# Token lists in 64-byte lines that carry the entry's weight, with bounded gathers and scatters

## The reference

```python
# x: 16 x 112 x 512, ctx: 16 x 375 x 512, mask: 16 x 375
x = x + attention(layernorm(x), ctx, mask)         # one head, softmax over the 375 rows of ctx
h = layernorm(x).reshape(-1, 512)                  # 1792 tokens
probs = softmax(h @ gate_weight.T)                 # 64 experts
top_val, top_idx = top_k(probs, 8)
top_val = top_val / sum(top_val)
# an expert that is nobody's first four may be replaced by a similar one (mapping of 64 entries)
for each of the 1792 * 8 = 14336 entries (token, expert):
    gu = h[token] @ gate_up[expert].T              # 512 -> 2 x 192
    y = (silu(gu[:192]) * gu[192:]) @ down[expert].T
    out[token] += top_val * y
x = x + out
```

## Time and profile before

| | us |
|---|---|
| median of 3 runs (lowest to highest) | 867.94 (867.48 to 870.99) |
| the profiled execution, its own time | 862.66 |
| its span, first to last instruction | 860.9 |
| PE busy in the span | 693.2 (81%) |
| DVE busy | 528.5 (61%) |
| ACT busy | 459.6 (53%) |
| POOL busy | 516.5 (60%) |
| moved by DMA | 196.36 MB |

### The profile page before, as it was taken

The page is one execution under the profiler, slowest core; times in us unless marked ns, Lnnn a source line. Parts: engine busy times, 40 slices in busy tenths (PEclk is TensorE's granted clock), DMA queues, the critical chain, the costliest instruction groups (busy, mean ns, idle before and its releaser), DMA issues. The chain is left out here.

```text
span 860.9 us, 15404 instructions
## 1 busy us (share of the span) xinstructions
PE 693.2 (81%) x4264; PEld 566.3 (66%) x4264; DVE 528.5 (61%) x1291; ACT 459.6 (53%) x900; POOL 516.5 (60%) x515
## 2 busy tenths in 40 slices
PE   5986868676017999999999999988998899999740
PEld 2544545343016999988888888877887778778630
DVE  4755736464125677776677777676776776776620
ACT  3543434232004676667666666767666676666520
POOL 2053535646716588888786676667676666666440
PEclk9997978885557999999999999999999999999965
DMA  8999986972047899999999999999999999999767
GB/s 274 351 333 157 214 189 132 182 201 64 2 143 232 192 256 264 248 259 263 248 245 276 269 271 275 286 242 273 279 248 253 269 265 265 256 249 260 152 120 164
DMA packets 103382, 196.36 MB, mean 228 GB/s; under 512 B 27697, under 2 KB 27825, under 8 KB 102850
## 3 DMA queue, kind: packets, MB, share of 16 engines
q1 hardware_dynamic: 70098, 121.70, 50.0%
q0 software_dynamic: 33200, 73.68, 40.7%
HBM read 147.23 MB, written 51.77 MB: 231 GB/s over the span
## 5 line engine op out<-in xcount | busy, mean ns | idle before, releaser
L1232 PE MATMUL bank<-xh,w1h 128*128 128x256 f32 (+7 forms) x768 | 227.7, 296 | 12.7 <-issue 4.5
L1233 PE MATMUL bank<-xl,w1h 128*128 128x256 f32 (+7 forms) x768 | 219.7, 286 | 0.0
L1234 PE MATMUL bank<-xh,w1l 128*128 128x256 f32 (+7 forms) x768 | 219.7, 286 | 0.0
L611 POOL DMA_INDIRECT xg<-normed_tokens,list x145 | 156.0, 1076 | 64.6 <-issue 49.3
L593 POOL DMA_INDIRECT list_table<-token,slot x112 | 107.5, 960 | 123.7 <-DVE token L781 91.3
L1232 PEld LDWEIGHTS bank<-xh,w1h 128*128 128x128 f32 x768 | 146.3, 190 | 17.2 <-issue 16.0
L635 POOL DMA_INDIRECT out_rows<-ys,list x73 | 117.4, 1608 | 62.1 <-ACT ys L1055 45.9
L635 POOL DMA_INDIRECT second_sum<-ys,list x70 | 111.9, 1599 | 59.7 <-ACT ys L1055 37.2
L1233 PEld LDWEIGHTS bank<-xl,w1h 128*128 128x128 f32 x768 | 146.5, 191 | 0.0
L1234 PEld LDWEIGHTS bank<-xh,w1l 128*128 128x128 f32 x768 | 146.3, 190 | 0.0
L925 DVE TENSOR_TENSOR xl<-bank,xh 128x448 fp32r<-128x448 f32 (+3 forms) x145 | 84.2, 617 | 90.0 <-ACT xh L1063 65.9
(11 more groups left out here) (205 smaller groups left out, 1123.9 us busy)
## 6 DMA issues: line engine op xcount, KB each, us to landing
raw<-in_w SPq DMA_DIRECT2D x195, 256.0 KB
raw<-in_w2a SPq DMA_DIRECT2D x65, 256.0 KB
ctxT_s<-in_ctxT SPq DMA_DIRECT2D x16, 768.0 KB
ctx_s<-in_ctx SPq DMA_DIRECT2D x16, 768.0 KB
raw<-in_w2b SPq DMA_DIRECT2D x65, 128.0 KB
second_sum<-zeros SPq DMA_DIRECT2D x18, 256.0 KB
x_in<-in_x SPq DMA_DIRECT2D x16, 224.0 KB
out_rows<-x SPq DMA_DIRECT2D x16, 224.0 KB
```

The source lines that it names most:

```text
L611: pool.indirect_dma_start(xg[u.on(XGS)][0:u.m, t, :], None, normed, bass.IndirectOffsetOnAxis(ap=lists[u.on(LISTS)][0:u.m, t:t + 1], axis= ...
L1232: pe.matmul(bank[m][:, 0:W], wh, mh, start=(c == 0), stop=False)
L1233: pe.matmul(bank[m][:, 0:W], wh, ml, start=False, stop=False)
L1234: mm = pe.matmul(bank[m][:, 0:W], wl, mh, start=False, stop=(c == DK - 1))
```

## The change

An entry of a list is now a line of 16 words (64 bytes): word 0 is the token's number, word 1 the weight of the entry. `place_entries` finds the weight of each of the 8 entries by comparing all 64 positions with the 8 sorted ones, and `spread` and `publish` move it along with the position. The column of weights beside the normalized row, its store and POOL's `weights` are gone; ACT takes the scale of a row from the list in SBUF. Gathers and scatters of the 63 units name a bound (`bounds_check=TOK - 1`), above which a row is left out; the three gather buffers are cleared once at the start so that rows left out hold numbers. A tile's rows are now consecutive entries of the list. The fills of the lists are 16 times larger for each entry; a first part (640 lines of each list) is issued in slot 1, the rest in slots 2 to 7, and `enter` of batch 5 waits for it. The core of the diff:

```diff
-LIST_PARTS = (2048, 192)
+LIST_PARTS = (2048, 16)
-FILLED = 2048
+FILLED = 1920
+LINE = 16
+BLANKS = 128
+NEAR = 640
...
-    table = nc.dram_tensor("list_table", (PAD_LIST + PADS, 1), I32, kind="Internal").ap()
+    table = nc.dram_tensor("list_table", (PAD_LIST + BLANKS, LINE), I32, kind="Internal").ap()
-    normed = nc.dram_tensor("normed_tokens", (ROWS, ROW), F32, kind="Internal").ap()
+    normed = nc.dram_tensor("normed_tokens", (ROWS, D), F32, kind="Internal").ap()
...
-            def store_weights(b):
-                sp.wait_ge(c_place, b.n * PLACE + 1)
-                sp.dma_start(normed[b.n * T:(b.n + 1) * T, D:ROW], wd[b.on(STORED)][:]).then_inc(wd_out[b.on(STORED)], 16)
+            def fill_lists(i, done):
+                quarter = P // (PADS // BLANKS)
+                source = blank[i % (PADS // BLANKS) * quarter:(i % (PADS // BLANKS) + 1) * quarter].rearrange("p n c -> p (n c)")
+                per_expert = table[0:PAD_LIST].rearrange("(e n) c -> e (n c)", e=E)
+                for e in range(0, E, quarter):
+                    sp.dma_start(per_expert[e:e + quarter, i * BLANKS * LINE:(i + 1) * BLANKS * LINE], source).then_inc(done, 16)
...
-                rows = table[bass.ds(at, u.rows), :].rearrange("(p t) c -> p (t c)", p=u.m)
+                rows = table[bass.ds(at, u.rows), :].rearrange("(t p) c -> p t c", p=u.m)
...
+            nc.gpsimd.memset(blank[:], 0).then_inc(cleared, 1)
...
+            for i in range(XGS):
+                nc.gpsimd.memset(xg[i][:], 0.0).then_inc(const_pool, 1)
...
             def gather(u):
                 split_wait(pool, list_in[u.on(LISTS)], (u.turn(LISTS) + 1) * 16)
                 split_wait(pool, xT_ps, u.tiles_freed(XGS))
-                split_wait(pool, wt_s, u.units_freed(XGS))
                 for t in range(u.nt):
                     pool.indirect_dma_start(xg[u.on(XGS)][0:u.m, t, :], None, normed,
-                                            bass.IndirectOffsetOnAxis(ap=lists[u.on(LISTS)][0:u.m, t:t + 1], axis=0)
-                                            ).then_inc(gathered[u.on(XGS)][t], 16)
+                                            bass.IndirectOffsetOnAxis(ap=lists[u.on(LISTS)][0:u.m, t, 0:1], axis=0),
+                                            bounds_check=TOK - 1, oob_is_err=False).then_inc(gathered[u.on(XGS)][t], 16)
...
-                yield from ch.link(v.tensor_scalar(wd[b.on(STORED)][:], pm[:], s8i[:], None, ALU.mult), tell=True)
...
-                yield from ch.link(v.max(placed8[:], placed[:]))
-                yield from ch.link(v.tensor_scalar(last8[:], column_is[:], placed8[:, TOPK - 1:TOPK], None, ALU.mult), tell=True)
+                yield from ch.link(v.max(entry8[:, 0, :], placed[:]))
+                wide = [T, TOPK, E]
+                yield from ch.link(v.tensor_tensor(of_entry[:], placed[:].unsqueeze(1).to_broadcast(wide),
+                                                   entry8[:, 0, :].unsqueeze(2).to_broadcast(wide), ALU.is_equal))
+                yield from ch.link(v.tensor_tensor(of_entry[:], of_entry[:], pm[:].unsqueeze(1).to_broadcast(wide), ALU.mult))
+                yield from ch.link(v.tensor_reduce(w8[:], of_entry[:], AX, ALU.add))
+                yield from ch.link(v.tensor_scalar(entry8[:, 1, :], w8[:], s8i[:], None, ALU.mult))
+                yield from ch.link(v.tensor_scalar(last8[:, 0, :], column_is[:], entry8[:, 0, TOPK - 1:TOPK], None, ALU.mult))
+                yield from ch.link(v.tensor_scalar(last8[:, 1, :], column_is[:], entry8[:, 1, TOPK - 1:TOPK], None, ALU.mult), tell=True)
...
+                yield from ch.link(v.tensor_copy(token[b.four][:, :, 1].bitcast(F32), bank[7][:, ENTERS:2 * ENTERS]))
...
-                act.wait_ge(wt_s, u.n + 1)
+                if u.loop:
+                    split_wait(act, kept, (u.n - STATIC + 1) * KEPT)
```

More of the change, by code:

```diff
@@ L464, in slot @@
                     fill(s)
-                batches(s, (2, store), (3, store_normed), (5, store_weights))
+                if s.n in FAR_AT:
+                    far = (FILLED - NEAR) // BLANKS
+                    for i in range(far * FAR_AT.index(s.n) // len(FAR_AT), far * (FAR_AT.index(s.n) + 1) // len(FAR_AT)):
+                        fill_lists(NEAR // BLANKS + i, far_filled)
+                batches(s, (2, store), (3, store_normed))
             phase1(sp, slot)
@@ L780, in publish @@
                 yield from ch.link(v.tensor_scalar(slot8[b.four][:], bank[7][:, 0:ENTERS], -1.0, float(PAD_LIST), ALU.mult, ALU.add))
[L781 removed]
+                yield from ch.link(v.tensor_copy(token[b.four][:, :, 1].bitcast(F32), bank[7][:, ENTERS:2 * ENTERS]))
+                yield from ch.link(v.tensor_scalar(token[b.four][:, :, 0], token[b.four][:, :, 0], 4 * T, None, ALU.add), tell=True)
                 ch.done()
@@ L1054, in y_out @@
                     act.wait_ge(y_ps, u.t0 + t + 1)
-                    a.activation(ys[u.on(2)][0:u.m, t, :], y_bank(u, t)[0:u.m, :], ACT.Copy,
-                                 scale=wt[u.on(WTS)][0:u.m, t:t + 1]).then_inc(ys_s, 1)
+                    of_row = over_wt[:] if u.loop else lists[u.on(LISTS)][0:u.m, t, 1:2].bitcast(F32)
+                    a.activation(ys[u.on(2)][0:u.m, t, :], y_bank(u, t)[0:u.m, :], ACT.Copy, scale=of_row).then_inc(ys_s, 1)
             def x_high(u, ts):
```

136 lines of the change are left out of this document (64 added, 72 removed).

## The result

The changed kernel takes 861.1 us (median of 20 runs, 851.0 to 877.9) against 867.1 us for the kernel before in the same comparison (20 runs, 860.6 to 873.7): a ratio of 0.991 [0.988, 0.993]. That is 6 to 8 us where 26 were forecast. (The bracket is a 95% interval; ratios leave out executions in a slower state, so they are not quite the quotients of the medians, and all profiles but nobound's are of executions in the usual state.) Later sets of runs fell on four chips, called I to IV here; on which chip this first comparison ran is not on record. On the fourth the kernel before takes 814 us and the changed one 832 (ratio 1.022 [1.019, 1.025]). So the sign of the result depends on the chip, and why it does is most of what follows.

The account below looks back on a forecast made before the run. Stage 2 was taken as bound by an ACT-DVE compute loop, stage 1 by completions held during POOL's stores. First gather 24 us earlier and stage 2's -2 made -26: 842 us against 867.9, range 824 to 884.

Parts of the forecast that it names:

- Stage 2: Gathers and scatters gain a bound on POOL, taken as 0; smaller transfers save bytes that nobody waits for.
- The 2 us for lighter first units: Start of stage 2: lighter traffic in the first units, -2 us.
- DVE in a slot: Stage 1: DVE's added operations lengthen each slot by 2.6 us, from 7.8 to 10.4 us.
- Fills: Stage 1: larger list fills delay the first store by 5.9 and 4.6 us; at least nothing, at most 15 us.
- The 10.5 us for bytes: Fills ahead of the first store: 5.9 us for those before slot 2's loads, 4.6 us for two slots more.
- Its upper bound: Most that the fills could cost: 15 us, for all 7.3 MB at 341 GB/s and some of SP's queue.
- the price of the held completions: Stage 1, during POOL's stores of entries: late PE completions cost 5.1 us a batch if still held, nothing if not.
- not held: Stage 1: 64-byte stores no longer delay PE's completions, so the 5.1 us a batch go; chance 0.53.
- the twelve slots: Stage 1, from batch 0's first store to batch 12's: 10.4 us a slot, -27.3 us in all.
- the first, in its milder form: Completions stay held, but DVE's longer slot keeps bursts apart: 12 us a batch, +5, 873 us; whole rival's chance 0.30.
- nothing net: Stage 1: holds shrink to some 2 us a batch and eat the gain, 860 to 872 us; chance 0.10.
- The last part: End of stage 1: POOL's last 28 stores to 222, plan done under them, 6 us more to first gather at 228.5.

Follow-up runs that it names:

- nobound: The changed kernel with gathers and scatters without a bound, so pad rows are moved again; 859.5 us, ratio 0.981 to the kernel before.
- pause_each: The kernel before with a small POOL memset (128x288) and a wait for it after each store of entries; 843.7 us, ratio 0.970.
- lines64: The kernel before with only the entries stored as lines of 64 bytes, without the rest of the change; 879.3 us, ratio 1.014.
- short8: The changed kernel, list pitch of 64 bytes kept, each store writing only the first 8 bytes of its line; 857.3 us, ratio 0.994.
- pause_end: The kernel before with one POOL memset (128x2560) and a wait for it after each batch's seven stores; 844.4 us, ratio 0.973.
- before_again: The kernel before, unchanged, profiled on chip IV; 815.1 us, ratio 1.000.
- tick32: The kernel before with a POOL memset of 128x32 and a wait for it after each store, on chip IV; 816.7 us, ratio 1.003.

## Why the prediction was wrong, step by step

**Stage 2** was right: next to no transfer was waited for (PE waits for gathered rows 6.9 us between 300 and 800 us, where it had 15.0), the stage's time is unchanged (608.3 and 608.4 us), and the bound cost nothing. The 2 us for lighter first units showed only on chip IV, if at all (605.5 and 605.7 us in the two profiles of the changed kernel there, 606.2 to 607.5 in the four of the kernel before).

**DVE in a slot** was right. The three operations of 112x512 take this, in the changed kernel (the row groups them by form, busy us and mean ns):

```profile
L775 DVE TENSOR_TENSOR of_entry<-of_entry,pm 112x512 f32<-112x512 f32 x16 | 11.0, 689 | 2.9 <-issue 2.4 <-DVE of_entry L773 0.5
L776 DVE TENSOR_REDUCE w<-of_entry 112x8 f32<-112x512 f32 x16 | 11.0, 686 | 1.3 <-DVE of_entry L775 0.8
```

0.68 to 0.69 us each, and undisturbed slots of 10.6 us (163.4 to 174.0 to 184.6 for `x`, L724) where 10.4 were forecast. (Behind `run` there are one product of 112x512, the reduction and three small operations; the other product stands ahead of it.)

**Fills** were put too high: first store at 57.6, not 62. The 10.5 us for bytes measured 5.8. Its upper bound was wrong in itself: 7.3 MB at 341 GB/s are 21 us, not at most 15.

**The failed step** is the price of the held completions, in the prediction's words: "Only the size and kind of the write tell the two apart", and from it "not held". What told them apart was what that sentence had excluded, how densely and how long POOL issues. At 4 bytes, one store in 1.26 us has 84.3 us of holds and one in 1.6 us has none (pause_each). Its "not held" was nearly met all the same, 21.3 us in place of 84.3, but by luck: DVE's longer slot did it, not the line of 64 bytes, which in lines64 is held 109.4 us. What was left of the holds is most of what is missing: the twelve slots gave 11.9 us and not 27.3 (on chip IV, where nothing is held, they take 125.3 us, as forecast). The prediction had the evidence ("All of these lie in stretches in which POOL stores entries without a pause"), and dropped it with "In stage 2 POOL issues as densely". There, between 300 and 800 us, POOL starts 257 indirect DMAs, one in 1.95 us, and never more than five in a row at its dense pace. The size rule that the prediction weighed (the Trainium skill, DMA: Bandwidth & Descriptors, Specifications: below 512 bytes a transfer becomes a read-modify-write) could not tell either, since 4, 8 and 64 bytes all lie below it. That 64 bytes would be no better than 8 or 4 is what the runs show (0.994 for short8, 0.991 for the changed kernel). Writes of 512 bytes and more at a store in 1.26 us were not tried, so a part of size above 64 bytes is not excluded.

**The rival that came nearest** is the first, in its milder form: DVE's longer slot "only keeps two bursts from joining, the long holds of 12 us go and a batch is 12 us". A batch was 11.7 us. It would have given 873; the cheaper fills (4.4 us) and slots that are 0.3 us shorter (twelve of them, 3.6 us) make that 865, near the 861 measured. By its time, the case "nothing net" (860 to 872) is what came.

**The last part** (28 stores, to 222, then "6 more") was wrong twice. The plan was not done under the stores. It took 12.3 us (223.9 to 236.2) because it, too, was held; the same instructions on the chip that holds nothing took 4.0 (205.7 to 209.7). And SP's eight weight DMAs stood ahead of the lists, from 237.99 to 243.94: 6.0 us.

On chip IV, where the assumption "not held" is true, the changed kernel takes 832 us, the forecast having been 842. The forecast of the changed kernel was nearly right for that chip; it was the kernel before that is another one there, 53 us faster.

## What to carry to other kernels

Before a stall is charged to a property of the work beside it (its size, its kind), list what else goes with it, its rate first; a pause is the cheapest experiment, and here, on a chip that holds, a memset of 0.35 us after each store gained more than the whole change. Where an edit speeds up one engine, ask whether a rest of another was doing something. And where waits end without a releaser that the profile knows, profile the same program on a second chip before building on them.

## What the runs showed of the hardware that was not expected

On three chips of four, completions are late while POOL issues indirect DMAs of 128 elements every 1.26 us: waits for them last up to 12.3 us where two bursts of seven join, and up to 7.4 us with single bursts and rests of 2.5 us and more (pause_end). It is so for stores of 4, 8 or 64 bytes and for gathers of 4; at one in 1.6 us (pause_each, one chip) none is late. It is not PE's alone. In the changed kernel's plan DVE waits for DVE itself, first rows, where on chip IV the same instructions follow on without a wait, second rows:

```profile
227.47 0.21 DVE L854 TENSOR_REDUCE rank<-ahead 64x1 f32<-64x64 f32 x1 [1.26 <-DVE cand L840]
228.10 0.22 DVE L841 MAX8 best<-cand 64x8 f32<-64x64 f32 x1 [0.42 <-DVE rank L854]
231.73 0.14 DVE L843 CAST bidxf<-bidx 64x1 f32<-64x1 uint32 x1 [1.92 <-remote]
```

```profile
207.07 0.21 DVE L854 TENSOR_REDUCE rank<-ahead 64x1 f32<-64x64 f32 x1
207.21 0.21 DVE L841 MAX8 best<-cand 64x8 f32<-64x64 f32 x1
207.88 0.15 DVE L843 CAST bidxf<-bidx 64x1 f32<-64x1 uint32 x1
```

For the row at 227.47 the trace has DVE's own update at 227.35, 1.15 us after the end of L840 at 226.20. So what is late is the semaphore's update, whoever sends it. The Trainium skill (Perfetto Trace Analysis, Tensor Engine Instruction) says that the reported end of a matmul is computed from its size, and the semaphore's update comes after it; that agrees with a PE that reads as finished while its waiters stand still, but names no cause for microseconds. Why POOL's rate should delay updates, and why chip IV shows nothing of it, stays open.

One rival to a cause in the chips is neither tested nor excluded: the profiler's own recording. The trace of the kernel before holds 11,035 updates of semaphores, that of the same program on chip IV 17,998; all twelve traces from chips I to III have 10,109 to 11,962, all six from chip IV 17,998 to 18,252. Of the 16 x 112 = 1792 updates that the stores of entries send, 539 are recorded before and 1785 in before_again. The loss alone does not hold anything up: pause_each loses a third as well, and so does stage 2, which takes 608.3 and 607.5 us on the two sorts of chip. But the chips on which records are lost are those on which completions are late, and every execution on record has a span of its own, so there is no time taken without the recording. Whether the 53 us between the chips would remain without it is not known.

Not tried: the memset of 0.1 us on a chip that holds, and a rate between 1.27 and 1.6 us there, so where it turns is unknown, and whether it is the rate or the instruction between. On chip IV that memset costs 2 to 3.5 us; on the others, if it is enough, it would let the kernel before come down to some 816 us (an estimate: tick32's time, since its slots are POOL's alone). The fastest version run on the chips that hold is, by its ratio, pause_each, at 0.970 of the kernel before (pause_end's 0.973 is not clearly apart); on chip IV it is the kernel before itself.
